# Constant multiplies in TensorE's pauses, in a sequence of Mamba, experts and attention

## The reference

```python
x = layernorm(x + mamba2_and_mlp(x))   # state-space scan, 4 heads of 64, state 128; gated MLP of 512
x = layernorm(x + moe(x))              # softmax gate, top 2 of 8 dense 128x128 experts
x = layernorm(x + attention(x))        # 16 heads of 8, sinusoidal relative bias times w_rel
x = layernorm(x + routed_ffn(x))       # top 2 of 8, capacity 512 rows an expert over all tokens
```

## Time and profile before

| | |
|---|---|
| median of 3 runs | 1607.4 us (1598.3 to 1607.55) |
| profiled execution, own time | 1609.85 us |
| its span | 1608.1 us |
| mean granted TensorE clock | 0.905 |
| TensorE busy | 1374.2 us (85%) |
| VectorE busy | 1092.4 us (68%) |
| ScalarE busy | 871.2 us (54%) |
| GpSimd busy | 267.9 us (17%) |

### The profile page before, as it was taken

One profiled execution on the slowest core, in us unless ns is written; L12 is line 12 of the kernel. 1 busy time (PEld: TensorE's weight loads), 2 busy tenths in 40 slices (PEclk: granted clock), 3 DMA queues, 4 the chain that ended last, 5 costly groups with the idle time before them and its releaser, 6 DMA issues. The chain is left out here.

```text
span 1608.1 us, 20695 instructions
## 1 busy us (share of the span) xinstructions
PE 1374.2 (85%) x7224; PEld 624.2 (39%) x7224; DVE 1092.4 (68%) x2093; ACT 871.2 (54%) x1762; POOL 267.9 (17%) x408
## 2 busy tenths in 40 slices
PE   5778898889979876899999999999999999982560
PEld 2455574566556554122223323233332333222340
DVE  5637559645864556888888888888888887923115
ACT  6436317423540222277777776777777777771225
POOL 2121121112110201000000110321104111053351
PEclk9779999977988868699999999999999999996795
DMA  4070000200020365110111110111101100000224
GB/s 115 10 170 14 1 1 14 96 1 0 1 97 1 48 98 187 53 21 2 21 21 22 38 21 2 36 33 38 22 11 27 25 2 2 1 7 24 62 83 156
DMA packets 45964, 63.51 MB, mean 39 GB/s; under 512 B 8706, under 2 KB 33869, under 8 KB 44022
## 3 DMA queue, kind: packets, MB, share of 16 engines
q1 hardware_dynamic: 42790, 57.97, 14.8%
q0 software_dynamic: 3072, 4.23, 0.8%
HBM read 33.07 MB, written 31.15 MB: 40 GB/s over the span
## 5 line engine op out<-in xcount | busy, mean ns | idle before, releaser
L579 PE MATMUL ps<-space 128*32 128x512 f32 (+5 forms) x4608 | 858.7, 480 | 47.8 <-DVE space L1825 21.2
L2059 DVE TENSOR_REDUCE smax<-ps 128x1 f32<-128x1024 f32 x512 | 605.1, 1220 | 114.2 <-PE ps L579 108.2
L1347 ACT ACTIVATE space<-ps 128x512 f32<-128x512 f32 x1024 | 555.4, 595 | 229.6 <-PE ps L579 229.0
L579 PEld LDWEIGHTS ps<-space 128*32 128x32 f32 (+5 forms) x4608 | 250.4, 110 | 630.8 <-ACT space L1347 328.4
L1445 POOL TENSOR_SCALAR eps_sum<-mv 128x4 f32<-128x4 f32 x32 | 7.3, 229 | 635.2 <-DVEq L1690 634.7
L579 PE MATMUL ps<-w_exp,space 128*128 128x128 f32 x512 | 91.2, 337 | 0.0
L1202 ACT ACTIVATE btok<-ps 128x128 f32<-128x128 f32 x32 | 8.9, 277 | 147.9 <-PE ps L579 64.7
L579 PEld LDWEIGHTS ps<-w_exp,space 128*128 128x128 f32 x512 | 78.6, 236 | 18.5 <-issue 18.5
L1784 DVE SCALAR_TENSOR_TENSOR space<-space,conv_w 128x512 f32<-128x512 f32 x96 | 71.2, 750 | 2.3
L1532 POOL DMA_INDIRECT expert_in<-space,slot x64 | 62.9, 983 | 37.6 <-issue 19.3
L1915 DVE TENSOR_TENSOR space<-xnT,ps 128x512 f32<-128x512 f32 x64 | 42.5, 685 | 38.5 <-PE ps L579 38.4
(11 more groups left out here) (247 smaller groups left out, 1467.8 us busy)
## 6 DMA issues: line engine op xcount, KB each, us to landing
q_rows<-space SPq DMA_DIRECT2D x24, 256.0 KB, 2.4
k_rows<-space SPq DMA_DIRECT2D x24, 256.0 KB, 2.9
space<-k_rows SPq DMA_DIRECT2D x16, 384.0 KB, 5.2
space<-q_rows SPq DMA_DIRECT2D x16, 384.0 KB, 6.8
expert_out<-x_all SPq DMA_DIRECT2D x2, 2048.0 KB, 21.5
space<-expert_out SPq DMA_DIRECT2D x4, 1024.0 KB, 8.8
v_rows<-space SPq DMA_DIRECT2D x4, 668.0 KB, 3.3
space<-v_rows SPq DMA_DIRECT2D x4, 668.0 KB, 6.7
```

What stands on the lines that cost most here:

```text
L579: return nc.tensor.matmul(out, lhsT, rhs, start=first, stop=last)
L1347: nc.scalar.activation(prob[:, QUAD * (step % PROB_SETS) + unit % QUAD, :], bank(STB + unit % 2), ACT.Exp)\
L2059: v.tensor_reduce(smax[:, N % 2, i:i + 1], ps[:, b0:b0 + 2, :].rearrange("p k n -> p (k n)"), AX.X, ALU.max).then_inc(S.s_max, 1)
```

## The change

A new helper `keep_clock(at, n)` issues n matmuls of the constant `ident16` with the constant `ones16` spread to 512 columns, into the PSUM bank `at`. Nobody reads what they write, and they wait for nothing. They stand at eleven places: per slot, in attention's run-up, in the last steps and ahead of the experts. `SEGB`, `OUTB` and bank 5 hold nothing that is still wanted at those places. Ahead of the experts TensorE first waits for a new semaphore `rows_leaving`, which GpSimd raises behind the 15th of its last 16 scatters, and for `ranked`, which VectorE now raises for the last sequence too.

```diff
+            def keep_clock(at, n):
+                for _ in range(n):
+                    mm(bank(at), ident16[:], ones16[:].unsqueeze(1).to_broadcast([P, HT, P]))
...
                 if p is not None:
                     pe.wait_ge(S.w_late, LATE_LOADED)
+                    if m is None:
+                        pe.wait_ge(S.l_ready, NT * B)
+                        keep_clock(SEGB, 20)
                     rows_turned_mlp(p)
+                    if m is not None:
+                        keep_clock(SEGB, 6)
...
                     decay_sums(m)
+                    if m == 0:
+                        keep_clock(5, 22)
                     chunk_front(m, 0)
                     chunk_after(m, 0)
                 if q is not None:
+                    if p is None:
+                        keep_clock(SEGB, 30)
                     rows_turned_tail(q)
...
                     if p is not None and c == HT:
+                        if m is None:
+                            keep_clock(SEGB, 24)
                         gates_turned(p)
+                        if m is not None:
+                            keep_clock(OUTB, 5)
                     if m is not None:
                         chunk_out(m, c)
...
                             gate_rows(p, 1)
+                        if m is not None and HT <= c < NT - 1:
+                            keep_clock(OUTB, 2)
                         for k in SUMS_AT.get(c, ()):
                             expert_sum(p, k)
+                            if k == E - 1:
+                                keep_clock(OUTB if m is not None else SEGB, 3)
...
+            keep_clock(SEGB, 14)
             pe.wait_ge(S.x1_ready, 2 * B)
...
             pe.wait_ge(S.oT_sb, 2 * B)
+            keep_clock(5, 16)
             for H in range(2):
                 kept_turned(B - 1, H, H)
...
+            pe.wait_ge(S.rows_leaving, 1)
+            pe.wait_ge(S.ranked, B)
+            keep_clock(5, 32)
             rows_turned(0)
...
                         .then_inc(S.scattered, 16)
+                    if b == B - 1 and r == NT * TOPK - 2:
+                        pool.sem_inc(S.rows_leaving, 1)
...
             ranked(B - 1, 5)
+            dve.sem_inc(S.ranked, 1)
             places_start()
```

More of the change, by code:

```diff
@@ L325, in build @@
             st_psum p_ready pv_done pv_evac pvT_psum o_recip o_ready tbank_free
-            oT_psum oT_sb proj_out res_bias x3_kept pick16_ready rank_psum slot_ready row_ids scattered rows_out picked ranked pool_step
+            oT_psum oT_sb proj_out res_bias x3_kept pick16_ready rank_psum slot_ready row_ids rows_leaving scattered rows_out picked ranked pool_step
             """.split()})
```

## The result

The changed kernel takes 1592.69 us (median of 13 runs, 1587.97 to 1599.21) beside 1607.55 us for the kernel before on the same chip (13 runs, 1597.61 to 1614.48): a ratio of 0.9909, 95% interval 0.9888 to 0.9929. The forecast was 1576. The gain is there, 15 us, but less than half of the 32 that I worked out. The profiled execution has a span of 1589.8 us for 1608.1 and a mean granted clock of 0.928 for 0.905, so 18.3 us are to be found in the traces.

The account below looks back on a forecast made before the run. TensorE bounds attention at full clock; about 215 us of the slots run at half clock. Terms sum to 34.8 us, less 3 for untreated pauses: 32 won, 1576 us forecast (1563 to 1586, chance 0.62; wider range 1561 to 1599).

Parts of the forecast that it names:

- Rival A: Slots: low-clock stretches move instead of going, half the 32 us is lost; 1592 us, between 1586 and 1598; chance 0.16.
- The step that failed: Slots 1 to 3: five multiplies behind `gates_turned` fit the 1.65 us pause free and prevent the low stretch behind it.
- first parts: Slots 1 to 3, turn of the gates to chunk_out of c = 5: 15.0 us each at full clock, 9.7 us won.
- Slot 4: Multiplies ahead of rows_turned_mlp(3) win 2.0 us, those ahead of gates_turned(3) net 5.7 us; together 7.7 us.
- Attention at nothing: 14 multiplies ahead of attention: neither delay nor clock moves the end of VectorE's maxima; 0, at most 1.6 us lost.
- Ahead of the experts: 32 multiplies end 3.5 to 4.8 us late, the first expert wins 3.5 us back: net loss of 0.6 us.
- the second parts: Slots 1 to 3, second half's bias rows to last expert sum: 22.1 us each at full clock, 14.1 us won.
- my 0.30 to 0.40: Slots' second parts: time lost per us at the low clock, from comparing slots 2 and 3 with slot 1.
- slot 0: 22 multiplies behind decay_sums, inside a pause of 6.19 us, win 1.5 us (0 to 1.9).
- the last steps: 16 multiplies in a pause of 4.85 us speed the transposes and routing multiplies: 1.9 us won (0 to 2.2).
- rival C: Everywhere: added multiplies don't raise the clock, cost 0.43 us each and overrun pauses by 34 us; 1641 us; chance 0.05.
- Rival B: The clock costs little because the lengthened multiplies lie in waits; 1594 to 1600 us; chance 0.10.

Follow-up runs that it names:

- e2: The changed kernel with all 221 added multiplies cut from 512 columns to one: 1643.28 us, ratio 0.9979 to the kernel before.
- e5: e1 plus a pair of added multiplies into bank 5 behind each of the 22 leading score pairs: 1579.67 us, ratio 0.9843 to the kernel before.
- e7: e5 plus added multiplies in most pauses left in the slots: 1566.21 us, ratio 0.9766 to the kernel before.
- e8: e7 with 64 instead of 32 added multiplies ahead of the experts: 1562.53 us, ratio 0.9737 to the kernel before.
- e1: The changed kernel with the pair at c = 4 in slots 1 to 3 replaced by five ahead of `gate_rows`: 1620.68 us, ratio 0.9835 to the kernel before.
- e6: e1 without the five multiplies behind `gates_turned`: 1582.87 us, ratio 0.9857 to the kernel before.
- e4: The kernel before plus only the five behind `gates_turned` and the pair at c = 4 in slots 1 to 3: 1648.24 us, ratio 1.0013.
- e10: The changed kernel without the five behind `gates_turned` and the pair at c = 4: 1624.85 us, ratio 0.9879 to the kernel before.
- e9: The changed kernel without any added multiplies in slots 1 to 3: 1636.78 us, ratio 0.9957 to the kernel before.

## Why the prediction was wrong

Faster was right, and that streamed columns keep the clock up was right too (e2); the size was not. Rival A's case (1586 to 1598) is where the time fell. Its reason, low stretches that move, has a share in single traces (e5, e7, e8), but what took most of the forecast gain is a pause that the change left open.

**The step that failed** is "Five behind gates_turned take 1.07 us; the pause there is 1.65 us, so they are free, and the low stretch that begins right behind that pause should not begin." It was worth 11.0 less 1.3 us and brought -2.5. The low stretch began behind the next pause, the 1.14 us ahead of `gate_rows`. I had read from slot 2 that it begins behind the pause of 1.65, and had looked neither at slot 1, where it began behind the wait of 1.14 already before the change, nor through the pauses that would be next. e1 fills that one too and finds 15.8 us less in the first parts than the change has (e5 12.7, e7 7.9, e8 12.8); e6 shows that the earlier one is needed as well; e4 and e10 show that the five alone bring nothing. My own figure for the part at full clock, 15.0, was too long by 0.8: it is 14.23 in e1, below the 14.3 of my own range, and the ten multiplies in it cost nothing, as `gate_rows` starts 6.03 us behind the turn of the gates in slot 1 in both traces.

**Slot 4** brought 3.3 us for 7.7. The front's 20 leave pauses of 1.53 and 1.28 us, as the 5.90 of the earlier trace rows was only the first of two waits, one ahead of each group of four transposes; it brought 0.5 us by the start of the `down` multiplies for the 2.0 forecast. The gates are followed by the unfilled `gate_rows` wait, and the low stretch behind it keeps only part of the gain: 18.94 us for 22.76 from the same place before (584.06 to 606.82, all of the gates and half the experts), 3.8 us for the 6.6 forecast there. With these pauses filled (e8) this part is 15.91 us at 1.00, but it was 15.86 at 1.00 in e5 as well, with the same 0.86 us left open. So what drops the clock here in the change and keeps it in e5 isn't shown.

**Attention at nothing** was wrong by 3.0 us. That neither the delay nor the clock moves the row maxima was right: they take 18.73 us after for 18.82 before. What I missed is that the low clock outlasts them into attention's own steps, and there each us of it costs 0.44 us by the estimate above; it lasted 3.7 us there before and 10.2 after. With a pair behind each score pair the maxima run at full clock, and then the clock fell behind the wait for `shift_rows` in e5 (2.54 us) and didn't in e7 (2.54 us) and e8 (2.48 us), so the length of the wait doesn't decide. What does, and why the return came later after the change than before, isn't settled.

**Ahead of the experts** the sign was wrong, +0.9 for the first expert in place of -0.6, from a wrong premise: the increment behind the 15th scatter doesn't wait for it. The 32 came 17.4 us ahead of the rows and cost nothing, but could not hold the clock. With 64 the first expert is 4.85 us, 3.1 less than before, near the 3.5 that I had put for it at full clock.

**What held**: the second parts (15.7 us for 14.1), though the rates came out above my 0.30 to 0.40: 1.56, 9.83 and 4.36 us for 3.3, 24.0 and 10.2 low us are 0.41 to 0.47 each. The 0.30 came from slot 3 against slot 1, which isn't the same work: it is 0.73 us shorter at full clock (21.06 for 21.79). And the 9.5 forecast for slot 2 rests on the 31.62 us of one execution, so that this term came true is partly luck. Also slot 0 (1.9 for 1.5), the last steps (1.6 for 1.9), and, against rival C, that the filling multiplies run at 0.21 us each where the clock is up. Rival B is refuted by e1 and e8: with more of the pauses filled the gain is 42 us here (2.6% of 1606.11). The Trainium skill ("TensorE: Matmul & The Clock Gate", Part 1) puts the ramp's loss under 1% of a typical span; the ratio of 0.9737 disagrees. In this kernel the clock falls and comes back again and again.

**The 3.4 us** between the traces' 18.3 and the medians' 14.9 is how the profiled executions lie: 1609.85 is 2.3 over the median of before, 1591.58 is 1.1 under that of after.

## What to carry over

When a pause in front of a slow stretch is to be filled, read on to the next wait ahead of that stretch, and read it in every repetition of the loop: here the two pauses in front of `gate_rows` had to be filled together, and the first of them alone was worth nothing. Even then a low stretch came back in some traces with the same instructions, so judge a filling by several traces and by the ratio, not by one ledger. Size each filling from the timeline, since each costs 0.21 us a multiply where it stands in no pause, and stop when the mean clock rises but the start of the next phase doesn't move. Try one place alone early; here 24 of 221 multiplies brought a gain that can't be told from that of all.

## What the runs showed of the hardware that was not expected

- The clock fell 0.8 to 1.6 us behind the end of short pauses: 1.65 us (slot 2 before), 1.14 us (slot 1, before and after), 0.86 us (slot 4 after). The length alone doesn't decide: behind the same 0.86 us it stayed at 1.00 in e5.
- It fell without such a pause too: in e8 it does so in the second expert step of slot 1 and the first of slot 2 (177.80 and 314.01), with no pause longer than 0.23 us behind five filling multiplies (15.78 and 15.74 us at 0.89, for 14.23 in slot 3). The same instructions in slot 3 kept it. What decides between the slots is open.
- An increment on GpSimd's queue that stands behind its 15th indirect scatter released TensorE during the sixth, 11.9 us before the 15th was over (1477.39 + 0.97 less 1466.49).
- On two of the chips run here the whole of attention is some 34 to 44 us longer in every traced kernel (815.69 us with 782.20 of TensorE busy in e9, for 777.5 to 782.1 with 769 to 773). In the trace of e1, TensorE, VectorE and ScalarE all stand still for 3 to 6 us at a time around GpSimd's indirect scatters (TensorE 2.77 us up to 1015.47 and 5.18 up to 1026.76), and the clock is at 0.50 between. Why these chips differ isn't known.
